# Attention and feed-forward in one block: the last two attention units woven into the first superblock, and the weight sums one step earlier

## What is computed

```python
q = rope((x @ Wq.T + bq).reshape(B, S, 16, 32)); k = rope(...); v = ...
att = softmax(einsum('bshd,bstd->bsht', q, k) / sqrt(32))   # over the 16 heads of one position
o = swapaxes(einsum('bsht,bstd->bshd', att, v), 1, 2).reshape(B, S, 512) @ Wo.T + bo
x = layernorm(x + o)
g, u = (x @ gate_w.T) * gate_s, (x @ up_w.T) * up_s         # 512 -> 1408
x = layernorm(x + ((silu(g) * u) @ down_w.T) * down_s)      # 1408 -> 512
```

## Time and profile before

| what | value |
|---|---|
| time, median of 3 runs (lowest, highest) | 1853.01 us (1849.86, 1856.38) |
| the profiled execution's own time | 1853.19 us |
| its span | 1851.4 us |
| TensorE busy | 1764.2 us, 95% |
| VectorE, ScalarE, GpSimd busy | 1383.3, 941.7, 806.7 us |
| chain that ended last | TensorE 49% of the span, VectorE 1% |
| mean granted TensorE clock | 0.976 of full speed |

### The profile page before, as it was taken

How to read it: one execution, slowest core, us unless ns; L and a number is a source line. 1 busy time by engine, 2 the same in 40 slices (tenths; PEclk the granted TensorE clock), 3 DMA queues, 4 the chain that set the end, 5 groups by cost and what they waited for, 6 DMA issues and landing times.

```text
span 1851.4 us, 40751 instructions
## 1 busy us (share of the span) xinstructions
PE 1764.2 (95%) x15138; PEld 1415.6 (76%) x15138; DVE 1383.3 (75%) x1978; ACT 941.7 (51%) x1458; POOL 806.7 (44%) x695
## 2 busy tenths in 40 slices
PE   6899999999999999997499999999999999999997
PEld 5777888888887888886378788787877878778785
DVE  6678988898889888988455667667666676666656
ACT  4445445554555455544254555455454555555453
POOL 5768888888888888886000110201102011020111
PEclk8899999999999999998699999999999999999999
DMA  6475777777776876778544353543525434254241
GB/s 192 97 159 136 160 171 168 157 153 173 174 158 149 177 172 157 150 174 208 164 154 140 97 180 111 172 154 115 174 93 182 161 127 149 89 198 144 85 165 68
DMA packets 447479, 278.20 MB, mean 150 GB/s; under 512 B 261440, under 2 KB 385984, under 8 KB 447424
## 3 DMA queue, kind: packets, MB, share of 16 engines
q1 hardware_dynamic: 447424, 277.50, 56.6%
HBM read 184.10 MB, written 93.32 MB: 150 GB/s over the span
## 4 chain that ended last, share of the span: by engine, by line
PE 49%; issue 1%; DVE 1%; ACT 0%; DMA 0%; POOLq 0%; POOL 0%; ACTq 0%; SPq 0%; DVEq 0%
PE bank_x L989 9%; PE bank_x L994 9%; PE acc L1004 4%; PE bank_y L994 4%; PE bank_y L989 4%; PE acc L1000 4%; PE bank_z L989 2%; PE bank_z L994 2%; PE bank_x L1004 2%; PE bank_x L1000 2%; PE bank_y L1000 1%; PE bank_z L1000 1%; PE bank_z L1004 1%; PE bank_y L1004 1%; DVE x_lo L1278 0%
## 5 line engine op out<-in xcount | busy, mean ns | idle before, releaser
L342 PE MATMUL ps_x<-w_hi,xc_hi 128*128 128x512 f32 x768 | 310.4, 404 | 17.4 <-POOL xc_lo L502 8.0
L1201 POOL TENSOR_TENSOR z<-z,xr 128x512 f32<-128x512 f32 x60 | 77.5, 1317 | 550.9 <-DVE z L1288 550.9
L343 PE MATMUL ps_x<-w_lo,xc_hi 128*128 128x512 f32 x768 | 306.7, 399 | 0.0
L346 PE MATMUL ps_x<-w_hi,xc_lo 128*128 128x512 f32 x768 | 306.5, 399 | 0.0
L989 PE MATMUL bank_x<-x_hi,slot 128*128 128x512 f32 x704 | 282.1, 401 | 19.9 <-DVE x_lo L1278 12.4
L994 PE MATMUL bank_x<-x_lo,slot 128*128 128x512 f32 x704 | 279.0, 396 | 0.0
L447 ACT ACTIVATE kX<-kT 32x512 f32<-32x512 f32 x256 | 160.9, 628 | 184.7 <-DVE kT L627 182.5
L523 POOL TENSOR_TENSOR qk_cos<-qk_in,rot 128x512 f32<-128x512 f32 x128 | 204.0, 1594 | 108.2 <-DVE qk_in L606 83.8
L529 POOL TENSOR_TENSOR qk_cos<-qk_cos,qk_sin 128x512 f32<-128x512 f32 x128 | 206.0, 1610 | 10.0
L342 PEld LDWEIGHTS ps_x<-w_hi,xc_hi 128*128 128x128 f32 x768 | 146.4, 191 | 56.6 <-issue 12.0
L989 PEld LDWEIGHTS bank_x<-x_hi,slot 128*128 128x128 f32 x704 | 133.2, 189 | 59.0 <-issue 16.0
(11 more groups left out here) (113 smaller groups left out, 3922.3 us busy)
## 6 DMA issues: line engine op xcount, KB each, us to landing
slot<-gu_hi SPq DMA_DIRECT2D x88, 896.0 KB, 5.0
xc<-x_cols SPq DMA_DIRECT2D x32, 512.0 KB, 5.4
v_rows<-v_in SPq DMA_DIRECT2D x32, 512.0 KB, 4.2
v<-v_rows SPq DMA_DIRECT2D x32, 512.0 KB, 5.2
res<-x_rows SPq DMA_DIRECT2D x64, 256.0 KB, 3.5
x_rows<-x_out SPq DMA_DIRECT2D x32, 512.0 KB, 2.8
x_cols<-x_turn SPq DMA_DIRECT2D x128, 128.0 KB, 2.6
wide<-x_cols SPq DMA_DIRECT2D x64, 256.0 KB, 5.1
```

Source lines behind the costliest of these rows:

```text
L342: pe.matmul(out, hi[:, k], w_hi[:, w, k], start=(k == 0), stop=False)
L343: pe.matmul(out, hi[:, k], w_lo[:, w, k], start=False, stop=False)
L346: last = pe.matmul(out, lo[:, k], w_hi[:, w, k], start=False, stop=(k == KE - 1))
L1201: pool.tensor_tensor(z[:, h, r], z[:, h, r], xr[:, r], ALU.add).then_inc(z_added[h], 1)
```

## The change

The two functions become one (`post_ln_layer`) with one block. Buffers of the feed-forward now lie over buffers of the attention phase, so a first writer waits for the last reader of what lay there (for instance the third `high_of_hid1` waits for the values' `pX` of unit 31 to be made).

1. The attention pipeline ends after step 32 on each engine. The output projection of unit 30 follows it. The rest moves into superblock 0: the values of unit 31 into chunk 3 and its output projection into chunk 4 on TensorE; softmax, residual, normalisation and transposes of units 29 to 31 into chunks 1 to 6 on VectorE, ScalarE and SyncE's queue. The down products of chunks 0 to 5 wait until chunks 5, 6 and 7, two in each.
2. GpSimd makes the first two sums of blocks of x1 (t3 and T1), which VectorE made.
3. The slabs of weights move up by one step: sums and loads of slab s in step s, high and low part of slab s-1 in step s. In step 1 the high and low part of slab 0, its stores and the loads of slab 1 stand at the step's end.
4. TensorE reads the flag and branches after the output projection of unit 30. There is no barrier between the phases.
5. The high and low parts of `hid1` use four slots for chunks 0 to 7, two before. In superblocks 1 to 7 the order of work is as before.

The diff, cut to its core:

```diff
@@ sync: slabs one step earlier, late in step 1
+            def ffn_slabs(s):
+                if (m := unit_of(s, 1, UNITS)) is not None:
+                    sp.wait_ge(f_lo_done, m + 1)
...
+                if (m := unit_of(s, 0, UNITS)) is not None:
+                    at_least(sp, f_lo_done, m)
...
+                if s != 1:
+                    ffn_slabs(s)
...
                     sp.wait_ge(biased[2], 2 * m + 2)
                     sp.dma_start(v_out2[m], v_in[:, :]).then_inc(v_stored, 16)
-
-            for s in range(UNITS + LAGS):
+                if s == 1:
+                    ffn_slabs(s)
+            for s in range(UNITS + 1):
                 step(s)
+            load_v(UNITS - 1)
...
+                if j in (3, 5, 7):
+                    m = UNITS - 3 + (j - 3) // 2
+                    store_x1(m)
+                    store_x1_cols(m)
+                if 4 <= j < 7:
+                    for k in range(4 * j - 16, min(4 * j - 12, NJ)):
+                        sp.dma_start(wd[:, k].bitcast(F32), dn_hi[:, E * k:E * k + E]).then_inc(dn_loaded[k], 16)
@@ gpsimd
+            def step(s):
+                late = isinstance(s, int) and s == 1
...
+                if (m := unit_of(s, 1, UNITS)) is not None and not late:
+                    low_of_slab(m)
...
+                if late:
+                    low_of_slab(0)
+                if (m := unit_of(s, 0, UNITS)) is not None:
+                    sums_of_slab(m)
+            unit_steps(pool, step, LAGS, UNITS, 1)
+            first_sums_of_x()
@@ tensor
-            unit_steps(pe, step, LAGS, UNITS, LAGS)
+            unit_steps(pe, step, LAGS, UNITS, 1)
+            pe.wait_ge(lo_reduced, 1)
+            pe.matmul(ps_x[0][0:1, 0:1], lo_top1[:, :], ones[:, :], start=True, stop=True).then_inc(lo_joined, 1)
+            project_heads(UNITS + 1, UNITS - 2)
...
+                            if first and j == 4:
+                                project_heads(UNITS + 2, UNITS - 1)
                             product(n, j - 1, P4)
                             product(n, j - 1, P3)
+                            if first and j == 3:
+                                weigh_values(UNITS - 1)
                             product(n, j, P6)
-                            if j > 1:
-                                down1(n, j - 2)
+                            for k in downs:
+                                down1(n, k)
...
+            pe.wait_ge(flag_set, 1)
+            with pe.If(pe.value_load(inexact[0:1, 0:1], min_val=0, max_val=1)):
@@ vector
+            low_of_heads(UNITS - 2)
...
+            subtract_top(UNITS - 1)
...
+            def rest_of_attention(j):
+                if j == 0:
+                    sum_t(0, 3)
+                    shift_of(UNITS - 3)
+                if j == 1:
+                    sums_of_prob(UNITS - 1)
+                    scale_prob(UNITS - 1)
+                if j == 2:
+                    add_residual(UNITS - 2)
+                    aggregate(UNITS - 2)
+                    turn_x1(UNITS - 3)
...
+                        if first and j == 2:
+                            turn_prob(UNITS - 1)
+                        if first and j == 3:
+                            low_of_heads(UNITS - 1)
```

More of the change, by code:

```diff
@@ new lines, in store, with others @@
+            def store(n, h):
+                for r in range(ROWS):
+                    if isinstance(n, int):
+                        sp.wait_ge(z_done[h], ROWS * n + r + 1)
+                    elif r == 0:
+                        sp.wait_ge(z_done[h], ROWS * n + ROWS)
+                    row = r if isinstance(n, int) else (r + 1) % ROWS
+                    sp.dma_start(out_supers[n, h, row], z[:, h, row]).then_inc(out_stored[h], 16)
+            def others(n, j):
+                now, last, next_ = super_of(n, 0), super_of(n, 1), super_of(n, -1)
+                tail = isinstance(n, int) and n == SUPERS
+                if j < 4 and now is not None and next_ is not None:
+                    load_raw(next_, 2 * j)
+                    load_raw(next_, 2 * j + 1)
+                if j == 2 and last is not None and not tail:
+                    load_rows(last, 1)
+                if j == 5 and now is not None:
+                    load_rows(now, 0)
+                if j == 7 and last is not None:
+                    store(last, 0)
+                if j == 10 and last is not None:
+                    store(last, 1)
+                if j == NJ and is_last(n):
+                    load_rows(n, 1)
+                if isinstance(n, int) and n == 0:
+                    rest_of_attention(j)
@@ new lines, in exact @@
+            def exact(n):
+                now, next_ = super_of(n, 0), super_of(n, -1)
+                for j in range(NJ + 1):
+                    if now is not None:
+                        if isinstance(n, int) and n == 0 and j == 0:
+                            load_slot(1, 1)
+                            load_slot(2, 2)
+                        if j > 0 and (j + 2 < NJ or next_ is not None):
+                            sp.wait_ge(p_done[P3], NJ * n + j)
+                            load_slot((j - 1) % 3, j + 2 if j + 2 < NJ else (j - 1) % 3)
+                    others(n, j)
@@ L334, in _ @@
+            sp.wait_ge(f_hi_stored, 2 * 16 * SLABS)
+            sp.wait_ge(f_lo_stored, 2 * 16 * SLABS)
+            sp.wait_ge(lo_seen, SLABS)
+            sp.wait_ge(flag_set, 1)
+            with sp.If(sp.value_load(inexact[0:1, 0:1], min_val=0, max_val=1)):
+                run(sp, general)
+            with sp.Else():
+                run(sp, exact)
+            for h in range(2):
+                sp.wait_ge(out_stored[h], 16 * ROWS * SUPERS)
         @block.tensor
@@ L425, in _ @@
+            pe.wait_ge(flag_set, 1)
+            with pe.If(pe.value_load(inexact[0:1, 0:1], min_val=0, max_val=1)):
+                products(True)
+            with pe.Else():
+                products(False)
         @block.scalar
@@ L498, in _ @@
+            run(act, super_step)
         @block.gpsimd
@@ L574, in _ @@
+            run(pool, super_step)
         @block.vector
@@ L687, in step @@
                 if (m := now4) is not None:
[L688 to L693 removed]
+                    turn_x1(m)
                 if (m := now1) is not None:
@@ L1347, in step @@
                     read_row(last, 1, 3)
-                    for r in range(T4):
+                    for r in range(ROWS):
                         add_row(last, r)
```

1458 lines of the change are left out of this document (748 added, 710 removed).

## The result

The changed kernel took 1810.62 us (median of 4 runs, 1806.44 to 1811.02) against 1852.28 for the kernel before on the same chip: ratio 0.9766, 95% interval 0.9754 to 0.9779. Its profiled execution took 1810.45 us, 1808.7 of it span.

The account below looks back on a forecast made before the run. TensorE was taken as the bound in both long stretches, leaving only the 69.1 us between them to win. Start +19.2 and border -28.6 gave -9.4 us: 1843.6 us, range 1830 to 1856.

Parts of the forecast that it names:

- Other edits: First x1 sums on GpSimd, four h1 slots, and steady superblocks keeping their order: 0 us for all three.
- The sum: Start and border terms together: +19.2 - 28.6 = -9.4 us.
- the sign that I set on superblocks 1 to 7: Feed-forward after the border: the forecast would be wrong if these superblocks were longer.
- The start: Slabs' work ahead of GpSimd's rotations delays unit 1 by 21.4 us; 19.2 us late, carried to the end.
- The border: Attention's end into superblock 0: lost time falls from 49.7 us to 13.2 plus 7.9, winning 28.6 us.
- Up to chunk 1: Border from the last scores to chunk 1's start: 25.5 us with 12.3 of work, lost 13.2.
- The idle time at the branch: TensorE after the projection of unit 30: 3.2 us idle, bounds 0 and 5.6.
- From chunk 1 on: Chunks 1 to 4 of superblock 0 take 41.3 us with 33.4 of work: lost 7.9.
- Rival C: Superblock 0: VectorE paces chunks 1 to 4, normalisations wait for stores; lost 17, not 7.9: 1853, no change; chance 0.18.
- A: Start and border: both terms hold as forecast, 1843.6 us, own range 1836 to 1850; chance 0.55.
- Rival D: Chunks 0 to 4: the clock stays at its lower level throughout; 1863 us, slower; chance 0.12.
- Rival B: Start: only the first delay, 8.5 us, reaches TensorE; 1833 us; chance 0.15.

Follow-up runs that it names:

- e6_before_in_step: The kernel before with only two unused tiles (480 bytes ahead of xc, 416 behind gu_scale), putting operand pairs 0 or 256 modulo 512 apart: 1811.40 us.
- e5_in_step: The changed kernel with unused tiles moving slot0 by 416 bytes and later tiles by 512, so large matmuls' operands share an address modulo 512 (some 256): 1800.79 us.
- e11_start2: e9_start with slab 3's store and slab 4's loads moved ahead of step 4's rope load on the queue: 1777.41 us.
- e9_start: e8_store with early slab work put back where the kernel before had it, slabs 0 to 2 in unused buffers, steps 3 and 4 catching up: 1791.46 us.
- e8_store: e5_in_step with the stores of x1's rows of units 29 to 31 issued one chunk earlier on the queue: 1792.81 us.
- e10_first_sums: e8_store with GpSimd's sums of slab 0 moved behind the rotations of unit 0: 1785.26 us.

## Why the prediction was wrong, by its own steps

**The step that failed** is "Other edits. [...] 0 for all three; if an address or a slot matters, the 6.6-us chunks would show it." The sum has no term for the new order of allocation: addresses were named as a doubt and put at nothing without a reason, and they were worth three quarters of the result. The chunks did show it (28 matmuls take 6.4 us at the fast pace, 6.5 at the slow one), and the sign that I set on superblocks 1 to 7, "longer", looked one way only. With both kernels in step, the change itself is e6_before_in_step to e5_in_step: 10.6 us by the medians and 8.0 by the spans of the two profiled executions, where the sum said 9.4. That this is close is luck: the start was taken some 7 us too dear and the border's gain some 6 us too large, and the two errors cancel. What is left of the 41.7 is the pace, about 31 us: 0.57 us in each of 27 steps of the loop (15.4) and 2.01 in each of 8 superblocks (16.1), by the periods in the table. The prediction took 0.235 us a matmul as the matmul's own time and carried it into the changed kernel; by the starts it was 0.233, and it was a time of that placement.

**The start** was right in mechanism, and its chain of waits is in the trace as written; the size was off. From the values of unit 2 (122.74 to 135.18) it is 12.4 us, not 19.2. This figure is good to a few us only: in the seven kernels with this same start these values begin between 130.7 and 137.3 us. Two terms were too large. The loads of slab 0 are issued at once behind the first rope load and the first rotation came at 31.69, 7.3 late, not 8.5; and the four stores took 2.7 us (47.02 to 49.7), not 4.5, so that unit 1's rotations were 17.3 late, not 21.4. TensorE then waited 1.02 us within its scores where it had lost 2.70 before, which paid back some. e11_start2, which removes the chain, gives 15.4 back.

**The border** was forecast at 28.6 and measured at 24.8 by the marks, 22.7 without the pace of one superblock. A small part of the miss is in the reading of before: chunk 1 starts at 933.53 there, not at 934.38, so the 69.1 us hold 22 matmuls of superblock 0 and not 20, which is 0.8 us too much of a gain. The two halves of the border erred in opposite ways. Up to chunk 1 I was too dear: 21.0 us from scores to chunk 1 (861.33 to 882.30), not 25.5. The idle time at the branch was 0.80, not 3.2; in eight of the nine experiments that have this branch it was 0.46 to 1.22 us, and 2.51 in e9_start, so it varies, and what the queue's row that gave 3.2 held beside it stays open. The Trainium skill (Runtime: NRT & Kernel Launch, section Instruction fetch mechanics) says that a taken branch out of the current window has to fetch its target first. The trace agrees in so far as TensorE does stand idle there, but that time also holds the read of the flag, and no run separates the two. The clock was back at the upper level at 869.2, with the projection still running, so the first products ran at full speed.

From chunk 1 on I was too cheap: from 882.30 to 1013.19 there are 130.9 us, less 105.9 that the same part takes in a later superblock and 6.9 of values and projection: 18.1 lost, not 7.9. Chunks 1 to 3 took 8.5, 8.9 and 10.7 us where I had 8.7, 9.2 and 10.7; chunk 4 took 15.7, not 12.7 (the wait of 2.4 us); and the wait of 4.5 us is in chunk 6, where the forecast lost nothing. The two waits behind x1_out's store are most of the difference, with the slow clock that follows each (10 matmuls at 0.43 behind the 4.5 us): e8_store took 8.0 back. Rival C named this ("ScalarE's normalisations wait for stores"), with 17 us lost, close to the 18.1 measured, and I gave it less weight than it had; it is an addition to A, not an alternative.

**Rival D** (lower clock all through chunks 0 to 4) did not come: between 882 and 1013 us 24 matmuls ran at 0.43 us, and the clock is 0.93 over the 69 us. **Rival B** fell with e10_first_sums and e11_start2.

## What to carry to other kernels

Where a large engine is at 100%, count its instructions per microsecond before taking their time as fixed; two paces in one trace, at fixed places of every superblock, pointed here at the operands. Put the tiles that TensorE reads together at one address modulo 256, with unused bytes if need be, before weighing any order of work. When a transfer is moved on a queue, read what stands ahead of it that waits: both the changed kernel's 4.5 us and my own e9_start lost their time there.

## What the runs showed of the hardware that I had not expected

- A matmul of 128x128 by 512 in this format takes 0.227 us from start to start when its two operands lie a multiple of 256 bytes apart, and 0.233 at the five other distances measured (means of the table, 227.1 to 228.6 and 232.8 to 233.6 ns). Where the distance changes within a stream, some four matmuls behind the change keep the old pace (in the changed kernel after each run of slot0 products).
- A store of 512 KB landed in 2.8 us in the median of the changed kernel, in 9.5 behind 1.9 MB on the same queue.
- TensorE stood idle for 0.80 us at the read of the flag and the taken branch over the whole code of the other case; over ten kernels this was 0.46 to 2.51 us.
- Scores in a step written out before or after the loop stall once for which the profile shows no releaser, five times in each trace, for 0.7 to 3.6 us each (10.9 us in all in the kernel before, 8.7 in e11_start2); inside the loop they do not. What sets this was not tried.
